# Layer two: the router's products between the last output products, and products of ones on TensorE

## What is computed

```python
Sim = (encoder_hc @ w1)[:, :, None] + (decoder_hq @ w2)[:, None, :] \
    + jnp.einsum('bid,bjd->bij', encoder_hc * w3, decoder_hq) + b_sim[0]
A = jax.nn.softmax(Sim, axis=2)
hq_hat = jnp.einsum('bij,bjd->bid', A, decoder_hq)
Batt = jax.nn.softmax(jnp.max(Sim, axis=2), axis=1)
hc_bar = jnp.einsum('bi,bid->bd', Batt, encoder_hc)[:, None, :]
hc_hat = jnp.broadcast_to(hc_bar, encoder_hc.shape)
feats = jnp.concatenate([encoder_hc, hq_hat, encoder_hc * hq_hat, encoder_hc * hc_hat], axis=-1)
hcq = feats @ W_qv + b_qv
```

```python
logits = jnp.einsum('bsd,de->bse', x, router_W) + router_b
probs = jax.nn.softmax(logits, axis=-1)
gates = jax.nn.one_hot(jnp.argmax(probs, axis=-1), N_EXPERTS) * probs
```

## Time and profile before

| | |
|---|---|
| median of 3 runs | 1627.48 us (1619.44 to 1636.02) |
| profiled execution, its time | 1621.11 us |
| profiled execution, its span | 1619.3 us |
| mean granted TensorE clock | 0.898 |
| TensorE busy | 1384.8 us (86% of the span) |
| VectorE busy | 861.7 us (53%) |
| ScalarE busy | 547.1 us (34%) |
| GpSimd busy | 418.2 us (26%) |

### The profile page before, as it was taken

How to read it: one execution, slowest core, us unless ns; L and a number is a source line. 1 busy time by engine, 2 the same in 40 slices (tenths; PEclk the granted TensorE clock), 3 DMA queues, 4 the chain that set the end, 5 groups by cost and what they waited for, 6 DMA issues and landing times. The chain is left out here.

```text
span 1619.3 us, 26329 instructions
## 1 busy us (share of the span) xinstructions
PE 1384.8 (86%) x8869; PEld 865.7 (53%) x8869; DVE 861.7 (53%) x2507; ACT 547.1 (34%) x1291; POOL 418.2 (26%) x729
## 2 busy tenths in 40 slices
PE   5799886995999859896994994756999999999998
PEld 2577663543787636555883773543444444344343
DVE  5577646874676523323663433754455546446425
ACT  2366555652577622223551331430101011011001
POOL 3687501104777100001344123620000000000000
PEclk9699987995799979995776997887999999999999
DMA  6766730004677468000001111232211302202200
GB/s 181 169 153 150 161 83 1 1 1 106 157 170 178 84 244 354 0 1 27 27 27 36 49 55 43 65 117 105 105 51 61 111 19 93 112 1 110 105 7 13
DMA packets 74720, 143.01 MB, mean 88 GB/s; under 512 B 13430, under 2 KB 53878, under 8 KB 64742
## 3 DMA queue, kind: packets, MB, share of 16 engines
q1 hardware_dynamic: 68038, 133.89, 28.4%
q0 software_dynamic: 3296, 6.76, 1.4%
q10 hardware_dynamic: 3264, 0.79, 0.3%
HBM read 99.33 MB, written 41.09 MB: 87 GB/s over the span
## 5 line engine op out<-in xcount | busy, mean ns | idle before, releaser
L2700 DVE TENSOR_TENSOR l3f_weighted_T<-l3f_w_e,l3f_xnT 128x512 f32<-128x512 f32 x128 | 88.4, 691 | 129.7 <-PE psum L2451 114.5
L2451 PE MATMUL psum<-l3f_weighted_T,w_l3f_q 128*128 128x512 f32 x256 | 133.7, 604 | 16.5 <-DVE l3f_weighted_T L2700 14.7
L2451 PE MATMUL psum<-l3f_weighted_T,w_l3f_k 128*128 128x512 f32 x256 | 131.6, 596 | 0.0
L2451 PE MATMUL psum<-l3f_weighted_T,w_l3f_v 128*128 128x512 f32 x256 | 131.3, 594 | 0.0
L2460 PE MATMUL psum<-l3f_weighted_T,w_l3f_o 128*128 128x512 f32 x256 | 124.3, 624 | 1.7 <-DVE l3f_weighted_T L2700 1.7
L2700 DVE TENSOR_TENSOR l3f_weighted_T<-l3f_w_e,l3f_oT 128x512 f32<-128x512 f32 x128 | 88.4, 692 | 57.2 <-PE psum L2460 30.3
L707 DVE TENSOR_REDUCE l1x_minus_max<-psum 128x4 f32<-128x512 f32 x128 | 84.7, 686 | 61.4 <-PE psum L360 60.5
L707 DVE TENSOR_REDUCE l0x_minus_max<-psum 128x4 f32<-128x512 f32 x128 | 84.4, 686 | 38.6 <-PE psum L360 37.9
L111 POOL TENSOR_TENSOR l3f_ln_rstd<-l3f_ln_mean_var,eps 128x4 f32<-128x4 f32 x8 | 2.0, 245 | 355.8 <-DVE l3f_ln_mean_var L104 355.8
L2460 PEld LDWEIGHTS psum<-l3f_weighted_T,w_l3f_o 128*128 128x128 f32 x256 | 39.3, 188 | 82.8 <-DVE l3f_weighted_T L2700 78.1
L2451 PEld LDWEIGHTS psum<-l3f_weighted_T,w_l3f_v 128*128 128x128 f32 x256 | 48.9, 191 | 61.8 <-issue 61.8
(11 more groups left out here) (486 smaller groups left out, 2991.5 us busy)
## 6 DMA issues: line engine op xcount, KB each, us to landing
l3f_w_e<-l3f_weights_scratch SPq DMA_DIRECT2D x32, 1024.0 KB, 4.7
sorted_x<-zeros SPq DMA_DIRECT2D x1, 16896.0 KB, 59.5
l0x_k_stack<-l0x_k_scratch SPq DMA_DIRECT2D x48, 192.0 KB
l0x_q_stack<-l0x_q_scratch SPq DMA_DIRECT2D x48, 192.0 KB
l1x_k_stack<-l1x_k_scratch SPq DMA_DIRECT2D x48, 192.0 KB
l1x_q_stack<-l1x_q_scratch SPq DMA_DIRECT2D x48, 192.0 KB
w_l2f_w<-in_l2f_w SPq DMA_DIRECT2D x2, 2048.0 KB, 13.2
l0x_k_scratch<-l0x_k_parts SPq DMA_DIRECT2D x16, 192.0 KB, 6.4
```

The costliest lines, as they stand in the source:

```text
L2451: ins = pe.matmul(bank[:, :], w[name][:, e, :], xe[:, e % 2, :], start=(e == 0), stop=(e == NE3 - 1))
L2700: dve.tensor_tensor(xe[:, e % 2, :], wE[:, g % 2, e, :], src, ALU.mult).then_inc(s_xe, 1)
```

## The change

`out` and `route` are called in halves. The first half of `out` has the bias product and three sequences, the second the fourth sequence; the first half of `route` has two sequences and stands between the halves of `out`, the second half has the other two and follows `out`. The router's products therefore stand ahead of `turn_attn`, not behind it. A new helper, `keep_streaming(n)`, issues n products of `ones_bf` with itself, 512 bf16 columns each, into `bankX2`, where nothing reads the result. It is called with 2 between the two halves of `similarity(s)` for s of 2 to 7, and with 3 between `attend(s)` and `weigh_tokens(s)` for the same steps.

```diff
                 ins.then_inc(s_s, 1)
                 if g >= 1:
                     pe.wait_ge(s_hb, g)
+                if 2 <= g:
+                    keep_streaming(2)
                 for c in range(GS):
                     ins = pe.matmul(bankM[:, c:c + 1], xnT[:, g % 3, seq(c)], w["l2x_w1"][:, :], start=True, stop=True)
...
+            def keep_streaming(n):
+                for _ in range(n):
+                    pe.matmul(bankX2.rearrange("p (c d) -> p c d", c=GS), ones_bf[:, :],
+                              bcast(ones_bf[:, :].unsqueeze(1), [P, GS, P]), start=True, stop=True)
+
+            def out(g, half):
+                if half == 0:
...
-                for c in range(GS):
+                for c in ((0, 1, 2), (3,))[half]:
...
-                ins.then_inc(s_o, 1)
+                if half == 1:
+                    ins.then_inc(s_o, 1)
...
-            def route(g):
+            def route(g, half):
...
-                for c in range(GS):
+                for c in (2 * half, 2 * half + 1):
...
-                ins.then_inc(s_lg, 1)
+                if half == 1:
+                    ins.then_inc(s_lg, 1)
...
-                if 1 <= s <= NG:
-                    out(s - 1)
+                for half in range(2):
+                    if 1 <= s <= NG:
+                        out(s - 1, half)
+                    if 2 <= s < NG + 2:
+                        route(s - 2, half)
                 if s < NG:
                     turn_attn(s)
-                if 2 <= s < NG + 2:
-                    route(s - 2)
-                if s < NG:
                     token_probs(s)
                     attend(s)
+                    if s >= 2:
+                        keep_streaming(3)
                     weigh_tokens(s)
```

More of the change, by code:

```diff
@@ L1511, in similarity @@
                 ins.then_inc(s_own, 1)
[L1513 to L1521, removed]
-                for c in range(GS):
+            def keep_streaming(n):
[4 more added lines that the diff above has]
+                if half == 0:
+                    if g == 0:
+                        pe.wait_ge(s_bias, 16 * NPART)
+                    pe.wait_ge(s_wc, g + 1)
+                    pe.wait_ge(s_haT, g + 1)
+                    if g >= 1:
+                        pe.wait_ge(s_x, g)
+                    pe.matmul(bankO.rearrange("p (c d) -> p c d", c=GS), ones_bf[0:NPART, :],
+                              bcast(bias3[:, :].unsqueeze(1), [NPART, GS, P]), start=True, stop=False)
+                for c in ((0, 1, 2), (3,))[half]:
                     pe.matmul(bankO[:, seq(c)], xnT[:, g % 3, seq(c)], wc[:, c, :], start=False, stop=False)
@@ L1565, in turn_h2 @@
                 ins.then_inc(s_h2p, 1)
-            def route(g):
[L1568 to L1573, removed]
-                for c in range(GS):
+            def route(g, half):
+                if half == 0:
+                    if g == 0:
+                        k.wait_weights(pe, "l2f")
+                    pe.wait_ge(s_hT2, g + 1)
+                    if g >= 1:
+                        pe.wait_ge(s_sh, g)
+                        pe.wait_ge(s_pos, g)
+                for c in (2 * half, 2 * half + 1):
                     ins = pe.matmul(bankL[:, c * NE2:(c + 1) * NE2], hT2[:, seq(c)], w["l2f_router"][:, :],
                                     start=True, stop=True)
-                ins.then_inc(s_lg, 1)
+                if half == 1:
+                    ins.then_inc(s_lg, 1)
             def count_before(g):
```

## The result

| | before | after |
|---|---|---|
| median | 1624.24 us (4 runs, 1619.44 to 1636.02) | 1604.9 us (4 runs, 1603.71 to 1607.88) |
| profiled execution, its time | 1621.11 us | 1603.9 us |
| profiled execution, its span | 1619.3 us | 1602.1 us |
| steps 2 to 7 | 81.58 us | 66.51 us |

The ratio is 0.9899, with a 95% interval from 0.9864 to 0.9935: 1.0% faster, and the interval leaves out no change. The medians differ by 19.3 us and the two profiled executions by 17.2. Of the 17.2, 15.1 lie in the six steps in which the ones run; the first turn of xn already started 0.8 earlier (742.89 against 743.73), which the change can't touch.

The account below looks back on a forecast made before the run. TensorE was taken as busiest, in a ring with VectorE, GpSimd and ScalarE. Steps of 6.45 + 4.71 = 11.2 us against 13.60 save 14.4 in six, from median 1627.48 to 1613 us; own range 1604 to 1622, widened to 1604 to 1633.

Parts of the forecast that it names:

- The step at full clock: One step of layer two's first loop, if the clock holds: 11.2 us against 13.60.
- o to h: From the end of the last output product to the start of the turn of h: 6.45 us, before 6.08.
- h to the next o: From the start of the turn of h to the end of the next last output product: 4.71 us, before 7.57.
- the wait for the diagonal: Ahead of the token probabilities, L1534 would briefly wait for L1873's diagonal, until now hidden by the router.
- VectorE did not become the bound: Row maxima on VectorE expected at 7.1 us after the last output product, before L1530 is due at 7.33.
- The term taken between 0.74 and 1.48: Row maxima, bias and first output pair at full clock: 0.8 us taken, 1.48 before.
- Step 8: The step after the six with ones: no change in length expected, or a gain of up to 2 us.
- rival 1: Clock still falls once in each of steps 2 to 7: about 1633 us, up to 1642; chance 0.14.
- Rival 2: Clock falls in some of steps 2 to 7, as they lose their fixed phase: 1623 us with three; chance 0.20.
- The rule that I weighed with rival 1: Transposes do not count as busy work for the clock as products do, so those behind the turn's start would lose it.

Follow-up runs that it names:

- the version with more: Kernel before's order, two ones ahead of the one-column products in every step, none behind attend, more ones where TensorE waits; ratio 0.9884 to the kernel before.

## Why the prediction was right, and where it was not

*The size.* Forecast 1613 from a median of 1627.48, that is -14.4; the six steps gained 15.07 and the medians 19.3. The median, 1604.9, lies just inside the range: the gain in the six steps was forecast, the other 4 us between the medians were not. Of 17.2 us between the profiled executions, 0.8 lies ahead of the loop and the remainder of 1.3 behind step 7; runs of each kernel scatter by more than that.

*The step at full clock.* Forecast 11.2, measured 11.14. From o to h 6.45 was worked out and 6.32 measured (801.14 to 807.46); from h to the next o 4.71 and 4.82 (to 812.28). The ones were priced at 0.22 and cost 0.22; the wait for the diagonal appeared where it was expected; VectorE did not become the bound. The term taken between 0.74 and 1.48 (row maxima, bias, first output pair), 0.8, measured 0.85 (808.36 to 809.21).

*Step 8* was to stay as long as it was, or gain; it grew from 11.49 (850.23 to 861.72) to 12.00. The clock falls among its outputs in both traces (856.75 to 860.16, and 0.86 above). But in the changed kernel the first half of the router stands among them, and it takes 0.71 us there at half clock (844.46 to 845.17); the half clock's price for that half was left out of the prediction's account of step 8.

*The rivals.* The clock did not fall in any of the six steps, so rivals 1 and 2 did not come about for this program. The rule that I weighed with rival 1, from the Trainium skill ("TensorE: Matmul & The Clock Gate", "Part 4: PE-mode transpose"), made me fear that the transposes behind h would lose the clock, and these traces don't show it: nine transposes in a row (807.46 to 808.57) ran in a stretch at 1.00. Whether they count for the clock at all is not settled by this; wide products stand on both sides.

*What was wrong is the reason for a fall.* The prediction took each step's own content to decide its clock: today the step loses it, since L1510 and its neighbours stand behind one-column products and ahead of 0.60 us of nothing; with ones both gaps are broken and the idling is gone, so it holds. The second half is borne out. In the eight traces of programs with wide ones, 35 of the stretches of steps 2 to 7 contain some, and 34 of them ran at 1.00; narrow products of the same time did not do it. The step that failed is the first half. The same instructions, with the same neighbours, the same 0.60 us of idle and no ones, run at full clock in 10.5 us in one execution and lose the clock in another. Of the 29 stretches in the order of the kernel before that hold no added products, the clock fell in 24; the five that kept it all stand behind a step with ones. In that order a step with a fall was always followed by another unless wide ones came in, and a free one mostly by a free one; step 4 of the second trace with ones in step 2, and step 7 of the first, fell behind free steps. Nor is the idling the reason: narrow products removed it, and the clock fell in every step. The router's move is not neutral either: by itself it kept the clock in three and four of six steps in its two traces and gained 0.8 to 0.9%. Rival 2's premise, that steps lose a fixed phase when ones are added, was nearer to this than the forecast's, but its price was for a kernel that falls at random, not for one that is caught.

*Left open.* Why a step without ones keeps the clock in one execution and not in another, and why moving the router alone is enough for most steps. That a step as long as its two stretches of clock together is what catches the kernel is argued, not shown: the steps with a fall in the two kernels with the router moved take 12.16 to 14.18, which fits; the steps with narrow products take 13.87 and more and fall every time, which doesn't; and no run changed the length of the step by itself. Of most kernels one trace was seen, so how often each is caught is not known; of the kernel before, the whole program's mean granted clock lies between 0.887 and 0.906 in the 31 and 25 runs recorded beside the experiments, and between 0.907 and 0.910 in the four of the changed kernel. The intervals of the variants that gained from 0.8 to 1.2% overlap, so which is best is open too.

## What to carry to other kernels

When every step of a loop runs half at half clock and half at full, suspect that it is caught: look at whether each step meets the clock's change at the same instruction, and whether the same step run at full clock is shorter. A few wide products in a step that is otherwise a mix of narrow ones and waits can hold the clock. They take 1.1 us a step here, but they stand mostly where TensorE would wait: a free step is 10.64 us with them and 10.48 without, both in the old order, against 13.65 caught. Take a second trace before crediting a cause: one program ran its steps at 10.5 us in one execution and at 13.5 in another.

## What was not expected of the hardware

- One program, two lengths of step: 10.48 and 13.42 to 13.59 us for the same instructions, with the clock at 1.00 and at 0.75 (ones in step 2 only, two executions).
- Filling all of TensorE's time with narrow products didn't hold the clock: 13.87 us busy of 13.87 with the clock at 0.75 on the mean. Nor did a busy TensorE raise it in step 1 of the version with more: 7.00 of 7.00 us at 0.50.
- Products of one column behind ones take slightly less from start to start than behind f32 products: 0.81 (804.30 to 805.11) against 0.90.
